# One GpSimd operation instead of two for the low halves of queries and keys in an attention and expert kernel

## The reference

```python
h = _layernorm(x, axis=-1) * (1 + ca) + sa
x = x + ga * _L0_attn_ref(h, w_qkv, w_out)
h = _layernorm(x, axis=-1) * (1 + cb) + sb
x = x + gb * _L0_ffn_ref(h, router_w, w1, w2)
```

```python
q = jax.nn.elu(apply_rope(q) * SCALE) + 1.0
k = jax.nn.elu(apply_rope(k) * SCALE) + 1.0
kv = kv + jnp.einsum('bhd,bhm->bhdm', kt, vt)
ks = ks + kt
denom = jnp.maximum(jnp.einsum('bhd,bhd->bh', qt, ks), 1e-06)
out_t = jnp.einsum('bhd,bhdm->bhm', qt, kv) / denom[..., None]
```

## Time and profile before

| what | before |
|---|---|
| median of 3 runs | 779.57 us (779.16 to 779.76) |
| span of the profiled execution | 776.0 us |
| TensorE busy | 714.8 us (92%) |
| VectorE busy | 628.2 us (81%) |
| ScalarE busy | 571.2 us (74%) |
| GpSimd busy | 518.5 us (67%) |
| granted TensorE clock | full, except half at about 33 to 37 us, 323 to 378 us, and at the very end |

### The profile page before, as it was taken

One profiled execution on the slowest core, in us unless ns is written; L12 is line 12 of the kernel. 1 busy time (PEld: TensorE's weight loads), 2 busy tenths in 40 slices (PEclk: granted clock), 3 DMA queues, 4 the chain that ended last, 5 costly groups with the idle time before them and its releaser, 6 DMA issues.

```text
span 776.0 us, 24871 instructions
## 1 busy us (share of the span) xinstructions
PE 714.8 (92%) x8105; PEld 549.7 (71%) x8105; DVE 628.2 (81%) x1494; ACT 571.2 (74%) x1108; POOL 518.5 (67%) x535
## 2 busy tenths in 40 slices
PE   8799999999999999845799999999999999999994
PEld 5467777777777776634677777777777777777772
DVE  4999999999999888778577777777777777777773
ACT  2799899999999998740476767777776767677772
POOL 5777777777777776547466666666666666666642
PEclk9999999999999999855799999999999999999997
DMA  6324344444443412310343343344333333443410
GB/s 226 113 67 133 110 135 120 131 120 139 124 140 116 151 64 67 120 48 8 96 77 69 71 73 74 76 70 79 70 75 69 77 69 76 76 72 76 72 21 1
DMA packets 52854, 69.27 MB, mean 89 GB/s; under 512 B 8864, under 2 KB 44080, under 8 KB 52736
## 3 DMA queue, kind: packets, MB, share of 16 engines
q0 software_dynamic: 18176, 27.06, 18.6%
q1 hardware_dynamic: 34560, 40.61, 16.9%
HBM read 46.50 MB, written 22.05 MB: 88 GB/s over the span
## 4 chain that ended last, share of the span: by engine, by line
PE 51%; DVE 2%; POOL 2%; issue 1%; DMA 1%; ACT 0%; POOLq 0%; DVEq 0%; ACTq 0%
PE hidden L1457 16%; PE bank L1475 15%; PE hidden L1459 8%; PE bank L1477 8%; PE bank L1292 2%; POOL mod_b L960 1%; PE bank L1309 0%; DMA xt<-ffn_rows,gi 0%; DMA out_dram<-x,si 0%; DVE stage L651 0%; PE bank L1300 0%; PE bank L1389 0%; POOL out_dram L1008 0%; DVE feat L652 0%; POOL mod_b L962 0%
## 5 line engine op out<-in xcount | busy, mean ns | idle before, releaser
L1457 PE MATMUL hidden<-qstT,w1hi_k 128*128 128x256 f16 x1136 | 197.9, 274 | 0.7 <-DVE qstT L755 0.7
L1459 PE MATMUL hidden<-qstT,w1lo_k 128*128 128x128 f16 x1136 | 193.6, 220 | 0.0
L1475 PE MATMUL bank<-w,amhi 128*128 x568 | 188.4, 379 | 0.1
L1477 PE MATMUL bank<-w,amlo 128*128 x568 | 154.8, 273 | 0.0
L1008 POOL DMA_INDIRECT out_dram<-x,si x71 | 115.2, 1622 | 38.8 <-issue 25.8
L791 DVE TENSOR_TENSOR amlo<-am,amhi 128x512 f16<-128x512 f32 x142 | 98.3, 693 | 49.2 <-ACT am L1168 49.2
L1457 PEld LDWEIGHTS hidden<-qstT,w1hi_k 128*128 x1136 | 111.7, 98 | 14.0 <-issue 1.1
L1459 PEld LDWEIGHTS hidden<-qstT,w1lo_k 128*128 x1136 | 111.6, 98 | 0.2
L1309 PE MATMUL bank<-wq,hT 128*128 128x512 f32 (+1 forms) x256 | 98.8, 511 | 1.3 <-DVE hT L524 1.2
L1475 PEld LDWEIGHTS bank<-w,amhi 128*128 128x128 f16 x568 | 55.6, 98 | 59.9 <-issue 0.4
L1167 ACT ACTIVATE amhi<-am 128x512 f16<-128x512 f32 x142 | 88.1, 620 | 0.3 <-DVE am L785 0.3
(11 more groups left out here) (219 smaller groups left out, 1783.6 us busy)
## 6 DMA issues: line engine op xcount, KB each, us to landing
stage<-in_L_ffn_w_dram SPq DMA_DIRECT2D x32, 512.0 KB, 4.3
xt<-in_L_attn_x_dram SPq DMA_DIRECT2D x32, 128.0 KB, 4.0
out_dram<-x SPq DMA_DIRECT2D x32, 128.0 KB, 3.7
ffn_rows<-h SPq DMA_DIRECT2D x32, 128.0 KB, 1.8
ffn_rows<-am SPq DMA_DIRECT2D x32, 128.0 KB, 4.2
am<-mod_rows SPq DMA_DIRECT2D x16, 128.0 KB, 4.0
mod_b<-mod_rows SPq DMA_DIRECT2D x8, 256.0 KB, 4.4
w<-in_L_wmod_dram SPq DMA_DIRECT2D x6, 256.0 KB, 4.6
```

The source lines that it names most:

```text
L1457: t.matmul(dst.rearrange("p (q n) -> p q n", q=2), w1s[0][k][g][:, w_], both, start=(k == 0), stop=False)
L1459: last = t.matmul(dst[:, P:2 * P], w1s[1][k][g][:, w_], both[:, 0, :], start=False, stop=(k == KT - 1))
L1475: t.matmul(y[:, :], ghi[:, m.p, c_m], w2s[mt // 2][:, bass.ds(w_, 2 * D)], start=(mt == 0), stop=False)
L1477: last = t.matmul(y[:, D:2 * D], glo[:, m.p, c_m], w2s[mt // 2][:, bass.ds(w_, D)], start=False, stop=(mt == MT - 1))
```

## The change

The two tiles `qst` and `kst` become two views of one tile `stacks`, behind which 48 more numbers per partition are reserved. The parts are now: queries high, low, high, empty; keys high, high, low, empty. So the product of the two low halves is no longer formed. The empty part is set to zero once, by a new memset in the constants of step 1. The low halves are written by one GpSimd operation over 512 numbers in place of two: its output view begins one part further on in the queries' stack and two parts on in the keys', which one regular step can reach because of the reserved numbers. ScalarE's and GpSimd's pieces that write the high halves, TensorE's transposes and matmuls, and all lists of orders stay as they were (the full diff also wraps the lists' lines in other places, with no entry changed).

```diff
+STACK = NH * 4 * HD
-        qst = sb("qst", [P, NH, 4, HD], F16)
-        kst = sb("kst", [P, NH, 4, HD], F16)
+        stacks = sb("stacks", [P, 2 * STACK + 3 * HD], F16)
+        qst, kst = (stacks[:, q * STACK:(q + 1) * STACK].rearrange("p (h c d) -> p h c d", h=NH, c=4) for q in range(2))
+        by_stack = stacks[:, 0:2 * STACK].rearrange("p (q h c) -> p q h c", q=2, c=4 * HD)
+        highs, nothing = by_stack[:, :, :, 0:HD], by_stack[:, :, :, 3 * HD:4 * HD]
+        lows = stacks[:, HD:2 * STACK + 3 * HD].rearrange("p (q n) -> p q n", q=2)[:, :, 0:STACK].rearrange(
+            "p q (h c) -> p q h c", c=4 * HD)[:, :, :, 0:HD]
...
-        POOL_CONST = 26
-        POOL_TWO, POOL_EROW = 47, 60
+        POOL_CONST = 27
+        POOL_TWO, POOL_EROW = 48, 61
...
                 link(g.memset(state[:, :, :, :], 0.0))
+                link(g.memset(nothing, 0.0))
...
                 wait(pool, a_["shk"], m.n + 1)
-                f = feat[:, :].rearrange("p (q h u d) -> p q h u d", q=2, h=NH, u=1)
-                g.tensor_tensor(qst[:, :, 1:4:2, :], f[:, 0].broadcast_to([P, NH, 2, HD]), qst[:, :, 0:3:2, :],
-                                ALU.subtract)
-                g.tensor_tensor(kst[:, :, 2:4, :], f[:, 1].broadcast_to([P, NH, 2, HD]), kst[:, :, 0:2, :],
-                                ALU.subtract).then_inc(a_["slo"], 1)
+                g.tensor_tensor(lows, feat[:, :].rearrange("p (q h d) -> p q h d", q=2, h=NH), highs, ALU.subtract)\
+                    .then_inc(a_["slo"], 1)
```

More of the change, by code:

```diff
@@ L60 @@
 ORDER_PE = (("aT", 4), ("ear", 3), ("sc1", 3), ("pj", 4), ("hT", 0), ("h2T", 6), ("Tk", 2), ("pv0", 3), ("v", 0),
-            ("Tq", 2), ("pv1", 3), ("lg", 6), ("state", 2), ("sc0", 2), ("qk", 0))
+    ("Tq", 2), ("pv1", 3), ("lg", 6), ("state", 2), ("sc0", 2), ("qk", 0))
 ORDER_DVE = (("st2", 5), ("st", 0), ("mv2", 5), ("mv", 0), ("ve", 0), ("f", 2), ("sl0", 3), ("nb", 0), ("rope", 1),
-             ("stl", 3), ("x1", 4), ("hTe", 0), ("sl1", 3), ("wlo", 1), ("vlo", 0), ("den", 3), ("rec", 3), ("at", 3))
+    ("stl", 3), ("x1", 4), ("hTe", 0), ("sl1", 3), ("wlo", 1), ("vlo", 0), ("den", 3), ("rec", 3), ("at", 3))
 ORDER_POOL = (("rs", 0), ("shk", 2), ("slo", 2), ("wb", 4), ("R", 1), ("xm2", 5), ("h2", 5))
 ORDER_ACT = (("exp", 2), ("sh0", 3), ("shq", 2), ("sth", 3), ("aTe", 4), ("xn", 0), ("sh1", 3), ("whi", 1),
-             ("kTs", 2), ("xn2", 5), ("vhi", 0), ("h2Te", 6), ("qTs", 2), ("lge", 6))
+    ("kTs", 2), ("xn2", 5), ("vhi", 0), ("h2Te", 6), ("qTs", 2), ("lge", 6))
 ORDER_SP = (("ldx", 0), ("modg", 6), ("modb", 7), ("so", 6), ("ro", 6), ("ld", 0), ("modgb", 6), ("gb", 6))
-OPENING_PE = {0: (("hT", 0), ("qk", 0), ("v", 0)), 1: (("hT", 0), ("mod1", 0), ("v", 0), ("qk", 0))}
+OPENING_PE = {0: (("hT", 0), ("qk", 0), ("v", 0)),
+    1: (("hT", 0), ("mod1", 0), ("v", 0), ("qk", 0))}
 OPENING_DVE = {0: (("st", 0), ("mv", 0), ("ve", 0), ("nb", 0), ("hTe", 0)),
-               1: (("st", 0), ("mv", 0), ("ve", 0), ("nb", 0), ("rope", 1), ("vlo", 1), ("hTe", 0), ("wlo", 1), ("vlo", 0))}
-OPENING_ACT = {0: (("xn", 0),), 1: (("xn", 0), ("vhi", 1), ("whi", 1), ("vhi", 0))}
+    1: (("st", 0), ("mv", 0), ("ve", 0), ("nb", 0), ("rope", 1), ("vlo", 1), ("hTe", 0), ("wlo", 1), ("vlo", 0))}
+OPENING_ACT = {0: (("xn", 0),),
+    1: (("xn", 0), ("vhi", 1), ("whi", 1), ("vhi", 0))}
 CLOSING = 28
@@ L87 @@
     ("den", 25), ("st", 30), ("rec", 25), ("ve", 29), ("at", 25), ("nb", 29), ("f", 27), ("sl0", 26), ("vlo", 28),
[11 rows of a table removed]
[1 row of a table added]
+    ("wlo", 27), ("ve", 30), ("f", 28), ("den", 26), ("rec", 26), ("vlo", 29), ("at", 26), ("stl", 27), ("nb", 30),
+    ("sl0", 27), ("rope", 29), ("hTe", 30), ("x1", 26), ("sl1", 27), ("f", 29), ("st", 31), ("st2", 26), ("mv", 31),
+    ("den", 27), ("rec", 27), ("mv2", 26), ("ve", 31), ("stl", 28), ("at", 27), ("sl0", 28), ("nb", 31),
+    ("rope", 30), ("vlo", 30), ("sl1", 28), ("wlo", 28), ("f", 30), ("hTe", 31), ("x1", 27), ("den", 28),
[6 rows of a table added]
 CLOSING_POOL = (("shk", 26), ("slo", 26), ("rs", 28), ("R", 27), ("xm2", 23), ("h2", 23), ("rs", 29), ("shk", 27),
@@ L104 @@
     ("h2", 29), ("rs", 35), ("xm2", 30), ("h2", 30), ("rs", 36), ("xm2", 31), ("h2", 31), ("wb", 31))
[L105 to L112, removed]
[4 rows of a table removed]
+CLOSING_ACT = (("exp", 26), ("sh0", 25), ("shq", 26), ("whi", 27), ("sth", 25), ("aTe", 24), ("sh1", 25),
+    ("kTs", 26), ("xn", 28), ("xn2", 23), ("qTs", 26), ("h2Te", 22), ("exp", 27), ("lge", 22), ("sh0", 26),
+    ("shq", 27), ("vhi", 28), ("sth", 26), ("xn", 29), ("aTe", 25), ("sh1", 26), ("xn2", 24), ("kTs", 27),
+    ("h2Te", 23), ("exp", 28), ("qTs", 27), ("vhi", 29), ("sth", 27), ("lge", 23), ("shq", 28), ("sh0", 27),
+    ("xn2", 25), ("whi", 28), ("aTe", 26), ("xn", 30), ("sh1", 27), ("kTs", 28), ("exp", 29), ("h2Te", 24),
+    ("qTs", 28), ("sth", 28), ("shq", 29), ("lge", 24), ("sh0", 28), ("whi", 29), ("vhi", 30), ("xn", 31),
+    ("xn2", 26), ("sh1", 28), ("kTs", 29), ("h2Te", 25), ("aTe", 27), ("exp", 30), ("qTs", 29), ("lge", 25),
+    ("shq", 30), ("sth", 29), ("sh0", 29), ("sh1", 29), ("aTe", 28), ("vhi", 31), ("kTs", 30), ("exp", 31),
+    ("qTs", 30), ("shq", 31), ("sh0", 30), ("aTe", 29), ("sth", 30), ("h2Te", 26), ("xn2", 27), ("sh1", 30),
+    ("kTs", 31), ("qTs", 31), ("xn2", 28), ("sh0", 31), ("lge", 26), ("sth", 31), ("aTe", 30), ("h2Te", 27),
+    ("sh1", 31), ("lge", 27), ("xn2", 29), ("whi", 30), ("h2Te", 28), ("aTe", 31), ("xn2", 30), ("lge", 28),
+    ("h2Te", 29), ("whi", 31), ("xn2", 31), ("lge", 29), ("h2Te", 30), ("lge", 30), ("h2Te", 31), ("lge", 31))
```

## The result

The changed kernel takes 781.25 us (median of 20 runs, 779.4 to 783.25), the kernel before 779.61 us (20 runs, 777.87 to 781.52): a ratio of 1.0019, 95% interval 1.0012 to 1.0027. It does 31 operations of GpSimd less (32 are gone, one memset is new) and is 0.19% slower, right at the edge of what can be told from no change. The forecast was 781.1 us. (One of the 29 launches of the kernel before in the first set of experiments took 846.49 us at a lower clock, and the ratios leave it out.)

What follows compares the result with a forecast made beforehand. Bound: a 9.46 us step loop through GpSimd's "slo", VectorE's own 9.19 us right below. Span 776.0 + 5.5 (middle) - 2.0 (opening) - 2.0 (closing) = 777.5 us, median 781.1; range 768.5 to 784.5.

Steps and rivals of the forecast that it cites:

- the cost of "slo": GpSimd's operation for the low halves: one of 1.16 us instead of two, ending 1.12 us earlier, so "Tk" stops waiting.
- The arrival of "xm2": GpSimd in each middle step: "xm2" comes 6.15 us behind "f", 0.20 us before VectorE's second "wlo" at 6.35.
- Who wins, and the price: Port shared by GpSimd and VectorE: "xm2" wins in nearly all steps and holds "wlo", costing VectorE 0.53 us.
- The sum of the middle: Steps 5 to 26 except the one at 80 us: 9.72 us each, 21 x 0.26 = +5.5 us.
- The opening: Before "xm2" exists: shorter "slo" and a "wlo" at 34 us free of GpSimd give -2.0 us (1.0 to 2.6).
- the prediction's own sign: Check on the opening: if it is not 2 us shorter, the estimate of it was at fault.
- The closing: From step 27: "nb" freed, last delay of 0.53 taken up, three or four chunks gain 0.1 to 0.2; -2.0 us.
- the held "nb" at 297 us: VectorE in the closing: held 0.87 us by the second operation of "slo", which the change removes.
- A: Rival: "xm2" does not win the place and VectorE's 9.19 us bind the step; 769 us, chance 0.20.
- B: Rival: "xm2" wins in some steps only, leaving opening and closing gains; about 775.6 us, chance 0.08.
- C: Rival: the step keeps its length, as ScalarE or TensorE binds in place of "slo"; 775.6 us, chance 0.07.
- D: Rival: the new operation lies on "nb" in each step, 0.87 us more for 22 steps; 800 us, chance 0.03.

Runs made afterwards that it cites:

- the first experiment: The changed kernel with one wait more: in the full steps "xm2" on GpSimd waits until "wlo" of the same step is done; 776.16 us, ratio 0.9872.
- eight memsets: The changed kernel with eight memsets of one number each ahead of every "xm2" on GpSimd; 773.35 us, ratio 0.9867.
- five memsets: The changed kernel with five memsets of one number ahead of every "xm2" on GpSimd; 773.83 us in one run, before 779.39.

## Why the prediction was right

- **What bound the kernel, and the cost of "slo".** Confirmed. The operation took 1.16 us, the waits of "Tk" and "kTs" went, and GpSimd's total fell by 35.2 us (37 said). Without the collision the step is 9.17 to 9.18 us (the first experiment, eight memsets), where the prediction had 9.19 for VectorE's own work.
- **The arrival of "xm2".** Said 6.15 us behind "f", 0.20 ahead of the second "wlo" at 6.35. Measured 152.09 - 145.95 = 6.14, and 0.20 ahead. That the step at 80 us could be carried over to all steps was the useful reading: it was the one step of before in which "wlo" was held so.
- **Who wins, and the price.** "xm2" wins in each of the steps at 0.20 us, even at 0.06, and the price is 1.22 - 0.68 = 0.54 us (0.53 said). The lock with a winner by order of start, which the Trainium skill states on its page SBUF — State Buffer, section "Who interferes with whom", is what the runs with three to eight memsets show: the held operation is either 1.22 or 0.68 us long, by who is first.
- **The sum of the middle.** +4.8 us where +5.5 was said. The step is 9.71 us, but 9.66 in every fourth step, and before's step from "f" of chunk 21 had been long already (9.76), so 20 steps lose 0.24 us on average, not 21 by 0.26. The term was sized 0.7 us too high; 0.3 of it is that one long step, which three other profiles with two operations there do not show (9.45 us).
- **The opening.** -2.1 us where -2.0 was said, measured alone at -2.1 (1.1 to 3.1). Its reason was half right: about 1.1 us are "slo", and 1.0 us is the stretch of half clock at 33 to 37 us, which the table of before lists and the prediction did not count. "wlo" at 34 us was to fall from 2.35 to 1.29 us; it took 1.89 (34.78 to 36.67), since the GpSimd operation beside it (on the tile `am`, 34.24 to 35.51) had not ended. The size was met by luck, and by the prediction's own sign (an opening not 2 us shorter for its reasons) the estimate was at fault.
- **The closing.** -1.07 up to chunk 30 where -2.0 was said (the run with the closing alone gave -1.2, -0.2 to -2.1, with an opening that was not before's). The 1.07 are 0.47 in the step from "f" of chunk 25, 0.18 in that of chunk 28 and 0.42 in that of chunk 29. The first has the size of the prediction's 0.53 for the last step's delay, but not its reason: it is the shorter "slo" of chunk 25, and comes without any delay too. Only one step gained 0.1 to 0.2, not three or four. And the prediction gave the held "nb" at 297 us the full 0.87. It got less, because the place beside "nb" was taken. VectorE and GpSimd of the changed kernel there:

```profile
301.08 0.47 DVE L507 SCALAR_TENSOR_TENSOR nb<-mv,rstd 128x2 f32<-128x2 f32 x1
```

```profile
300.80 0.74 POOL L883 TENSOR_TENSOR h<-h,mod_b 128x256 f32<-128x256 f32 x1
```

"xm2" follows directly behind "slo" there, and moved up by the time that "slo" gave free. It holds "nb" to 301.54, so "nb" takes 0.47 us, not 0.15: 0.55 us are gained instead of 0.87. It is the same mechanism as in the middle, and the prediction had not asked what moves up into the gap.
- **The sum.** -2.1 + 4.8 - 1.1 = +1.6 us, against +1.5 said. Two terms were off by 0.7 and 0.9 us in opposite directions, and 1.0 of the third was the clock: the mechanism of the middle is shown, and that the sum came within 0.1 us is luck. (The 781.1 of the prediction is 777.5 + 3.6; with the 3.5 that it names it would be 781.0.)
- **The rivals.** A is what the kernel would be if "xm2" lost: 769 us was said, and the experiments that make it lose stand at 0.987 to 0.989 of before, 769 to 771 us. The point from which it decides was said to be a shift of 0.2 us; it is 0.15 to 0.17 (from 0.20 ahead to 0.053 to 0.032 ahead). B is what five memsets give. C and D did not come: the step changed its length, and "nb" stays at 0.15 us in the middle (median of 20).

What stays open: the changed kernel's profile has 0.65 us more behind chunk 30 than before's. From "f" of chunk 30 to the last addition of the stage it took 35.6 to 36.8 us in the profiles with one operation in the closing, and 36.8 in this one (36.0 before). The clock falls to half 17 to 20 us behind that "f", at another point in each profile. Whether that is the reason is not shown.

## What to carry to other kernels

When a change shortens an engine's work, write down what arrives earlier and what it lands on: here a GpSimd operation that came 0.3 us earlier against VectorE took the shared port from the busiest engine, and 1.3% of gain became 0.2% of loss. Look in the trace of before for a step in which the shortened part was not the bound; it shows the new state. And where two engines meet at a port, decide the order yourself: one wait that lets the idle engine go second was worth nothing before the change and 1.5% after it.

## What was not expected of the hardware

The order of starts decides at a few hundredths of a microsecond and nothing softens it: with "xm2" recorded 0.053 us ahead VectorE's operation took 1.22 us, at 0.032 us ahead 0.68 us. That bound is not at zero: GpSimd needs a recorded lead of somewhere between 0.032 and 0.053 us to win.

A memset of one number per partition on GpSimd takes 0.10 us in the trace, but they overlap: three in a row moved the next operation by only 0.11 us, and eight by 0.27 (from 0.20 ahead to 0.07 behind), 0.03 to 0.04 us each. Small operations in a row are a fine-grained delay.

A short stretch of half clock can fall into a busy opening, and where it falls differs between executions of one kernel: the changed kernel had one at 11.8 us in its first profile and none in its second. Ahead of the first "f" it cost 1.2 to 1.8 us (19.8 to 20.4 against 18.6), in before's step from chunk 1 to chunk 2 0.9 us, in the run with three memsets at the same place 0.1 to 0.4 (28.39 for the opening against 27.97 to 28.31), and at 301.6 us 1.06. Near 33 to 38 us it was there in three of the four profiles with two operations and in one of the nine with one. That it moves with the length of the opening is only seen, not shown. Differences of 1 us between two profiles are to be read with the clock beside them.
